# The attention's bias moved from a VectorE copy of the residual into the value product, as a bf16 row in three parts

## What is computed

```
h  = relu(layernorm(x))
for each of three layers:
    h = leaky_relu(mean_of_neighbours(h) @ Wl.T + b + h @ Wr.T, 0.01)
x1 = x + h
g  = relu(layernorm(x1)) @ W
a_s, a_d = g @ att_src, g @ att_dst
e  = leaky_relu(a_s[src] + a_d[dst], 0.2);  alpha = softmax of e over each node's edges
out = x1 + sum over edges (alpha * g[src]) + bias
```

## Time and profile before

| | us |
|---|---|
| median of 3 runs | 3276.03 |
| lowest and highest | 3267.15, 3280.86 |
| the profiled execution: time | 3295.59 |
| the profiled execution: span | 3293.9 |
| PE, PEld, DVE, ACT, POOL busy | 2073.8, 1809.0, 1983.1, 1403.5, 1834.4 |

### The profile page before, as it was taken

The page is one execution under the profiler, slowest core; times in us unless marked ns, Lnnn a source line. Parts: engine busy times, 40 slices in busy tenths (PEclk is TensorE's granted clock), DMA queues, the critical chain, the costliest instruction groups (busy, mean ns, idle before and its releaser), DMA issues. The chain is left out here.

```text
span 3293.9 us, 51342 instructions
## 1 busy us (share of the span) xinstructions
PE 2073.8 (63%) x12372; PEld 1809.0 (55%) x12372; DVE 1983.1 (60%) x8287; ACT 1403.5 (43%) x3736; POOL 1834.4 (56%) x1801
## 2 busy tenths in 40 slices
PE   0002677777784776767658989898864444555444
PEld 0001566666673665656547777777754444545444
DVE  7973444444452454544437888888856666666666
ACT  0494233333331222222214555555555555555555
POOL 1003666666646666666646666666635555555553
PEclk9999888899896888878879999999977777777777
DMA  3495566666664666666656777777754444555444
GB/s 98 149 324 170 164 187 197 186 191 189 194 191 114 202 194 192 194 195 199 187 166 188 223 214 219 222 219 220 221 159 118 120 126 123 130 130 126 124 123 111
DMA packets 600937, 576.11 MB, mean 175 GB/s; under 512 B 83405, under 2 KB 561311, under 8 KB 600608
## 3 DMA queue, kind: packets, MB, share of 16 engines
q1 hardware_dynamic: 395104, 311.69, 32.8%
q0 software_dynamic: 57360, 106.10, 14.8%
q10 hardware_dynamic: 148176, 155.01, 13.4%
HBM read 378.74 MB, written 207.75 MB: 178 GB/s over the span
## 5 line engine op out<-in xcount | busy, mean ns | idle before, releaser
L608 POOL DMA_INDIRECT rows<-tab,idx x1323 | 1364.4, 1031 | 880.7 <-issue 355.3
L829 PE MATMUL bank<-mask,rows 128*128 128x128 f32 (+1 forms) x3528 | 707.5, 341 | 160.8 <-issue 129.2
L1233 DVE TENSOR_TENSOR sage<-bank,sage 128x256 f32<-128x256 f32 x588 | 248.4, 423 | 862.8 <-remote 530.2
L829 PEld LDWEIGHTS bank<-mask,rows 128*128 128x128 f32 x3528 | 605.6, 215 | 227.7 <-issue 183.3
L608 POOL DMA_INDIRECT rows<-tab_c,idx x441 | 447.3, 1014 | 430.4 <-PE bank L939 175.8
L701 ACT ACTIVATE sage<-bank,b_col 128x256 f32<-128x256 f32 x392 | 184.9, 472 | 797.2 <-remote 433.5
L1213 DVE TENSOR_SCALAR mask<-iota,dcol 128x256 f32<-128x256 f32 (+1 forms) x1323 | 408.7, 342 | 0.0
L929 PE MATMUL bank<-ident,mask 128*128 128x128 f32 x784 | 171.2, 358 | 376.4 <-ACT mask L761 269.9
L929 PEld LDWEIGHTS bank<-ident,mask 128*128 128x128 f32 x784 | 124.2, 186 | 390.8 <-ACT mask L761 278.1
L781 ACT ACTIVATE sage<-cut_w,ed 128x256 f32<-128x256 bf16 (+1 forms) x441 | 184.7, 472 | 302.4 <-DVE ed L1424 287.4
L854 PE MATMUL bank<-sage,wcat 128*128 128x256 f32 x784 | 268.9, 429 | 50.8 <-issue 45.8
(11 more groups left out here) (212 smaller groups left out, 3476.5 us busy)
## 6 DMA issues: line engine op xcount, KB each, us to landing
sage<-inv_d SPq DMA_DIRECT2D x588, 128.0 KB
turned<-sage ACTq DMA_DIRECT2D x392, 128.0 KB
tab<-sage ACTq DMA_DIRECT2D x392, 128.0 KB
sage<-turned SPq DMA_DIRECT2D x392, 128.0 KB
tab_c<-sage ACTq DMA_DIRECT2D x196, 132.0 KB
own_w<-tab_c SPq DMA_DIRECT2D x196, 132.0 KB
tab<-sage ACTq DMA_DIRECT2D x49, 512.0 KB, 4.4
xin<-tab SPq DMA_DIRECT2D x196, 128.0 KB
```

The lines of the kernel that those rows point to most:

```text
L608: eng.indirect_dma_start(out=rows[:, s.win[w], 0:width], out_offset=None, in_=table, in_offset=bass.IndirectOffsetOnAxis(ap=idx[:, s.w + w ...
L829: m = eng.matmul(to[:, a:b], rows[:, s.win[w], 0:D], mask[:, s.mw[w], c:c + b - a], start=(w == 1), stop=(w == 2))
L1233: eng.tensor_tensor(agg_t[:, o.r, :], ps[:, 0:TILE], own_t[:, o.v, :], ALU.add).then_inc(S["sum_v"], 1)
```

## The change

The bias goes into g: ahead of each of the two f32 matmuls of the value product PE does a bf16 matmul of three rows of ones against `bg_row`, 130 columns, whose first 128 are the attention's bias in three bf16 parts and the last two zeros. DVE's `x1b` is gone; SP stores `x1` itself, out of its ring of four, and waits for `x1_v`. DVE, ahead of writing a slot of `x1`, now waits for the store that last read it. `bg_row` is made in the preparation.

```diff
@@ phase_3 on SP
-                        eng.wait_ge(S["x1b_v"], o.t + 1)
-                        eng.dma_start(pair_rows(x1_d, o.t), x1b[:, o.b, :, :]).then_inc(S[f"stx{o.b}"], 16)
+                        eng.wait_ge(S["x1_v"], o.t + 1)
+                        eng.dma_start(pair_rows(x1_d, o.t), x1[:, o.r, :, :]).then_inc(S[f"stx{o.r}"], 16)
@@ phase_3 on PE
                     for j in range(2):
-                        m = eng.matmul(ps_g[o.b][:, j * TILE:j * TILE + D + 2], h_t[:, o.b, j * P:(j + 1) * P],
-                                       wg[:, :], start=True, stop=True)
+                        to = ps_g[o.b][:, j * TILE:j * TILE + D + 2]
+                        eng.matmul(to, ones_b[0:SP, :], bg_row[:, :], start=True, stop=False)
+                        m = eng.matmul(to, h_t[:, o.b, j * P:(j + 1) * P], wg[:, :], start=False, stop=True)
@@ preparation on DVE: the parts of a bias, now for two layers
+            def parts_of(layer, to):
+                op(eng.tensor_copy(b_rest[:, 0, :], b_bc[0:SP, layer, :]))
...
+            parts_of(LAYERS - 1, b_row[:, 0, :])
+            op(eng.tensor_copy(b_row[:, 1, :], b_sum[:, :]))
+            op(eng.memset(bg_row[:, D:D + 2], 0.0))
+            parts_of(LAYERS, bg_row[:, 0:D])
+            eng.sem_inc(S["b_v"], 1)
@@ phase_3 on DVE
                     wait(eng, S["h_a"], NSG + f.t - RING + 1)
+                    wait(eng, S[f"stx{f.r}"], 16 * f.uses(RING))
                     eng.tensor_tensor(x1[:, f.r, :, :], act[:, f.b, :, :], xin[:, f.r, :, :], ALU.add
                                       ).then_inc(S["x1_v"], 1)
...
                     scale(b, NSG + b.t)
-                    wait(eng, S[f"stx{b.b}"], 16 * b.uses(2))
-                    eng.tensor_tensor(x1b[:, b.b, :, :], x1[:, b.r, :, :],
-                                      b_bc[:, LAYERS, :].unsqueeze(1).to_broadcast([P, 2, D]), ALU.add
-                                      ).then_inc(S["x1b_v"], 1)
                     shift(b, NSG + b.t)
```

More of the change, by code:

```diff
@@ L205, in build @@
         b_row = sb("b_row", [SP, 2, D], BF16)
+        bg_row = sb("bg_row", [SP, D + 2], BF16)
         is_part = sb("is_part", [SP, SP])
@@ L275, in build @@
         x1 = sage[:, 4352:5376].rearrange("p (r j d) -> p r j d", r=RING, j=2)
-        x1b = sage[:, 5376:5888].rearrange("p (b j d) -> p b j d", b=2, j=2)
         h_c = sage[:, 5888:6400].rearrange("p (b j d) -> p b j d", b=2, j=2)
@@ L354, in build @@
                  "sum_v t_v l_v z_a n_cp sq0 sq1 sq2 sq3 sq4 sq5 sq6 b_v ln_v ln_a rs_v nmr_v h_a tr_done ht_cp dense_done wg_done g_cp st0 st1 st2 "
-                 "st3 x1_v x1b_v stx0 stx1 "
+                 "st3 x1_v stx0 stx1 stx2 stx3 "
                  "one_v turn cl0 cl1 cl2 cl3 cl4 cl5 cl6 cl7 cl8 cl9 cl10 cl11 cx0 cx1 cx2 cx3 cx4 cx5 cut_v sc_a zm_done "
@@ L492, in fast_sync @@
                 eng.wait_ge(S[f"st{r}"], 16 * (LAYERS * NG // RING))
-            for b in range(2):
-                eng.wait_ge(S[f"stx{b}"], 16 * (NG // 2))
+            for r in range(RING):
+                eng.wait_ge(S[f"stx{r}"], 16 * (NG // RING))
             def phase_c(s):
@@ L1193, in fast_vector @@
                 op(eng.tensor_scalar(is_part[:, k:k + 1], part[0:SP, 0:1], float(k), None, ALU.is_equal))
[L1194 to L1203, removed]
+            def parts_of(layer, to):
+                op(eng.tensor_copy(b_rest[:, 0, :], b_bc[0:SP, layer, :]))
+                for k in range(SP):
+                    op(eng.tensor_copy(b_part[:, k, :], b_rest[:, k % 2, :]))
+                    if k < SP - 1:
+                        op(eng.tensor_tensor(b_rest[:, (k + 1) % 2, :], b_rest[:, k % 2, :], b_part[:, k, :],
+                                             ALU.subtract))
+                op(eng.tensor_scalar(b_sum[:, :], b_part[:, 0, :], is_part[:, 0:1], None, ALU.mult))
+                for k in range(1, SP):
+                    op(eng.scalar_tensor_tensor(b_sum[:, :], b_part[:, k, :], is_part[:, k:k + 1], b_sum[:, :],
+                                                ALU.mult, ALU.add))
+                op(eng.tensor_copy(to, b_sum[:, :]))
+            parts_of(LAYERS - 1, b_row[:, 0, :])
[3 more added lines that the diff above has]
+            eng.sem_inc(S["b_v"], 1)
             def masks(g, to, io, done, w, value):
```

## The result

The kernel with the change takes 3289.05 us (median of 15 runs, 3277.08 to 3302.89), the kernel before, beside it on the same chip, 3273.34 us (15 runs, 3267.15 to 3280.86). The ratio is 1.0048 [1.0036, 1.0061]: 15.7 us more, where 70 us more had been predicted. It lies outside the range of 3300 to 3400 us, and of the cases it is nearest to "the cover holds", which had a chance of 0.07.

What follows compares the result with a forecast made beforehand. PE was taken as closest to the bound, taking turns with DVE. Packed 2.90 + 0.69 = 3.59 us plus 0.365 staying surplus gives 3.955 against 3.60: +0.355 a step, +70 us over 196 tiles, 3276 to 3346; range 3300 to 3400.

Steps and rivals of the forecast that it cites:

- the cover holds: Rival: PE's surplus of 0.70 us a step is all waiting and absorbs the rows; time stays at 3276 us; chance 0.07.
- PE's packed step: PE's own work of a `phase_3` step without a gap: 2.90 us plus 0.69 for the rows, 3.59 us.
- The split: Price of one row matmul on PE in `phase_3`: 0.345 us, with 0.055 us taken for its 130 columns.
- What has no releaser ... are PE's own, and stay: 0.365 us: PE's gaps ahead of L829 and inside groups, and slow-clock stretches in `phase_3`, stay: 0.365 us a step.
- if the gaps without a releaser go as well: Sign of being wrong: in the `phase_3` profile after, PE's gaps that nothing is named as ending vanish too.
- DVE: Dropping L1307 between reciprocal and `nmr` frees 0.16 us a step, worth nothing with a busy PE.
- over 1 us: Sign: DVE's idle time in `phase_3` grows to over 1 us a step, ending with PE.
- SP and the new wait: SP's store no longer holds its queue (42.3 us of 400), without gain; DVE's new wait for a store is safe.
- The preparation: Making the row delays DVE's masks by about 3.06 us, hidden behind the DMAs: costs nothing.

Runs made afterwards that it cites:

- four rows: The change with a further row matmul of zeros behind each value product, four a step; ratio 1.0284 to the kernel before.
- slow sets: The second, third and fourth sets of runs, in which the kernel before takes 3272.7, 3302.7 and 3305.0 us.
- the change without rows: The change without its two row matmuls, so the attention's bias is left out of the output; ratios 1.0007 and 0.9989 to the kernel before.
- fast set: The first set of runs, in which the kernel before takes 2763.6 us.
- rows alone: The kernel before with only the two row matmuls added, their row all zeros; ratio 1.0375 to the kernel before.
- one gather less: The kernel before without the last gather of each tile's rows in `phase_3`, matmuls unchanged; ratio 0.9623.
- one row: The change with a row matmul ahead of the first value product only; ratios 1.0136 and 1.0038 to the kernel before.
- rows side by side: The change with both row matmuls ahead of both value products; ratio 1.0064 to the kernel before.
- thin loads: The kernel before with SP's three loads of `phase_3` a quarter as wide, gathers unchanged; ratio 1.0045.

## Why the prediction was wrong, step by step

**PE's packed step: right.** 3.59 us predicted, 3.60 measured. The two rows were priced at 0.69 us from the starts around L889, and cost 0.71. The rule of the "Back-to-back issue gap" (the Trainium skill, "TensorE: Matmul & The Clock Gate"), 57 ns for one, does not hold for a lone row of three partitions between f32 matmuls, where 355 ns were measured. The split was right too: 0.30 us of turning and 0.055 of columns. That two rows side by side turn only once was not thought of, and this change does not put them so.

**"What has no releaser ... are PE's own, and stay: 0.365 us": this step failed.** Hardly any of it stayed: the step became 3.63 us over a packed step of 3.60, and not 3.955. PE's idle time of 42.9 us in 400 fell to 2.4, and the granted clock rose from 0.97 to 1.00 as PE no longer stopped. The 15.7 us of the medians are 0.08 us for each of the 196 tiles, not 0.355. The prediction had named this as a sign of being wrong: "if the gaps without a releaser go as well". The mistake was to take a gap for which the profile names no cause for a property of the engine that stands in it. The kernel with four rows, with 4.01 us in every step and none of these gaps, shows that PE has no such stops of its own.

**What was not looked at: who else was idle at the same time.** I read DVE and ACT as the others with whom PE takes turns. But no engine was full. POOL, too, stood for 37.7 + 37.3 us of 400 in pauses, at waits for slots, and with its work and issue it needs only 2.93 us of a step of 3.60. Where no engine is full, something between them sets the pace, and added work on one engine can fill its idle time first: here 0.71 us of it moved the step by 0.01 to 0.07 us between the traces of three sets. What these waits are made of in the slow sets is open.

**DVE: right in size and worth.** Reciprocal to `nmr` is 0.17 us (0.21 predicted), and the change without rows gives 0.9989 [0.9976, 1.0001] and 1.0007 [0.9998, 1.0016] in two sets. DVE's idle time ahead of the own-rows sum grew from 45.5 to 71.3 us, 0.64 us a step and less than the "over 1 us" that went with a step of 3.955; most of it ends with "remote" and not with PE.

**SP and the new wait: right.** 2.4 us at L486 in place of 42.3, and no gain from it; DVE's new wait does not show, since its idle time ahead of `x1` is 7.5 us in both.

**The preparation: right.** The masks end 3.2 + 0.3 us later and PE's first work starts 0.5 us later, but the first sums start at 298.09 where it was 298.48: hidden.

**The chances.** "The cover holds" was priced at no change, 15.7 us off, and its reason was the true one: PE's surplus was waiting. It was given 0.07 because only 17.2 us of the idle time stood at L904 and little had a named end. Those names were no evidence. What was luck: PE's new packed step, 3.60, ends within 0.05 us of the floor in the result. In the fast set, where the floor is 3.06, the same rows cost 104 us, more than my forecast.

## What to carry to other kernels

An engine's idle time with no named cause in a pipelined loop is slack until shown otherwise. Before adding work to the fullest engine, work out its packed step with the new work and set it against the average step of today: the new step is about the larger of the two, not a sum. Here the fullest engine had 0.7 us of surplus in 3.6; added work cost little up to that and its full price beyond. Treat a near tie as a coin toss, above all if the program is to run where the rest of the loop is faster. Before calling a feeding engine the bound, look how long its product lies ready: gathers that end 30 us ahead of their use are not late, whatever their pauses. Put short matmuls of few partitions side by side, or give them 128 partitions of mostly zeros: 0.11 us in place of 0.355.

## What was not expected of the hardware

The same kernel took 2763.6, 3272.7, 3302.7 and 3305.0 us in four sets, the first and the last of them under the same chip number. It is not the TensorE clock where PE is never idle: that is 1.00 in the middle of `phase_3` both in rows alone (fast set) and in one gather less (slow set). In the first layer, from 290 to 880 us, the granted clock is 0.88 in the kernel before and 0.96 in rows alone, beside 440 and 474 us of busy PE in 590; whether that is a cause or goes with the idle time is not shown. The difference goes with pauses of POOL at its waits for a slot: 59.4 us in 400 in the first layer of the one, none in the other. What makes POOL resume so late is open; leaving out a gather made it vanish in `phase_3`, and so mostly did four rows.

A lone bf16 matmul of three partitions between f32 ones costs 0.355 us, of which 0.30 is the turn, and four of them in three runs 1.12 us. The same matmul with 128 partitions costs 0.11 us.

Near the floor the two limits add a little. In the third and fourth sets one row, rows side by side, thin loads and the change lie 12, 22, 16 and 31 us above the kernel before, 0.06 to 0.16 us for each tile, though PE had room for the first two and the third has less to load. Why is open. It is also open which part of a gather holds the loop up in the slow sets, its work on POOL or its transfer, since one gather less takes away both. The kernel before and the whole change were not traced in the fast set; the change without rows and the rows alone stand in for them.
